# Attention and expert routing on one core: batch 1's q and k projected in three periods, the last x pass two periods later, q's weights applied after the turn, and a ten-round threshold search

## The reference

```python
xn = _layernorm(x, axis=-1)                       # x: 16 x 512 x 256
x = x + attention(xn) + ffn(xn)

# attention: 16 heads of 16, q and k with an RMS norm and a learned weight
q = rms_norm(proj(Wq), qn_w); k = rms_norm(proj(Wk), kn_w); v = proj(Wv)
attn = softmax(einsum('bhnd,bhmd->bhnm', q, k) * scale)
out = einsum('bhnm,bhmd->bhnd', attn, v) @ Wo.T

# ffn: 8 experts; each takes the C = T // 8 best of the tokens that are left
norm = layer_norm(feat, ln_g, ln_b); scores = norm @ centroids.T
for e in range(E):
    s = where(taken, -inf, scores[:, e]); _, idx = top_k(s, C); taken[idx] = True
routed = feat[concatenated idx]; h = layer_norm(routed, ln_g, ln_b)
h = gelu(h @ w1[e] + b1[e]) @ w2[e] + b2[e]       # 256 -> 1024 -> 256
out = routed + h, put back at each token's place
```

## Time and profile before

| | |
|---|---|
| three runs | 1201.72, 1202.34, 1205.91 us; median 1202.34 |
| the profiled execution | 1197.54 us, its span 1195.8 us |
| PE | 1063.0 us busy (89%) |
| DVE, ACT, POOL | 801.6 us (67%), 747.8 us (63%), 737.7 us (62%) |
| first block | to about 765 us |

### The profile page before, as it was taken

The page is one execution under the profiler, slowest core; times in us unless marked ns, Lnnn a source line. Parts: engine busy times, 40 slices in busy tenths (PEclk is TensorE's granted clock), DMA queues, the critical chain, the costliest instruction groups (busy, mean ns, idle before and its releaser), DMA issues. The chain is left out here.

```text
span 1195.8 us, 20979 instructions
## 1 busy us (share of the span) xinstructions
PE 1063.0 (89%) x7286; PEld 693.9 (58%) x7286; DVE 801.6 (67%) x1836; ACT 747.8 (63%) x966; POOL 737.7 (62%) x798
## 2 busy tenths in 40 slices
PE   4394999889999999999999999379999999999997
PEld 3251545445444444544454435268888888888887
DVE  6263687647787878687868778166676767667573
ACT  1173778678888878887888777154454444555442
POOL 5756679837667766776677631326665666655662
PEclk9697999989999999999999999679999999999999
DMA  3736687567686767667857680322424424243232
GB/s 113 165 66 150 113 201 159 127 127 141 138 155 154 125 139 163 147 130 148 159 153 127 147 166 19 128 76 46 123 49 111 110 41 124 45 119 83 64 45 27
DMA packets 84042, 138.17 MB, mean 116 GB/s; under 512 B 12496, under 2 KB 38352, under 8 KB 81872
## 3 DMA queue, kind: packets, MB, share of 16 engines
q1 hardware_dynamic: 56064, 104.63, 39.6%
q0 software_dynamic: 12288, 16.79, 8.6%
q10 hardware_dynamic: 15568, 15.21, 4.9%
HBM read 86.25 MB, written 50.33 MB: 114 GB/s over the span
## 5 line engine op out<-in xcount | busy, mean ns | idle before, releaser
L551 ACT ACTIVATE prob<-S 128x1024 f32<-128x1024 f32 x512 | 498.5, 1022 | 147.2 <-PE S L392 146.3
L392 PE MATMUL S<-stq,stk 64*128 64x512 f32 x1024 | 200.0, 458 | 55.8 <-DMA stk<-parts 40.4
L407 PE MATMUL pv<-prob,v 128*17 128x512 f32 x2048 | 247.3, 600 | 1.3 <-DVE oT L666 1.2
L1166 PE MATMUL dn<-w,hid 128*128 128x256 f32 x1536 | 194.1, 285 | 7.4 <-DVE hid L1332 7.2
L1166 PEld LDWEIGHTS dn<-w,hid 128*128 128x128 f32 x1536 | 188.1, 192 | 11.7 <-DVE hid L1332 10.0
L1154 PE MATMUL up<-nT,w 128*128 128x512 f32 x768 | 180.9, 395 | 12.8 <-DVE w L1268 10.5
L392 PEld LDWEIGHTS S<-stq,stk 64*128 64x128 f32 x1024 | 83.8, 186 | 180.3 <-ACT prob L551 111.2
L1154 PEld LDWEIGHTS up<-nT,w 128*128 128x128 f32 x768 | 145.2, 191 | 44.6 <-DVE w L1268 11.9
L1232 ACT ACTIVATE act<-up,b 128x512 f32<-128x512 f32 x128 | 87.9, 687 | 125.2 <-PE up L1154 124.1
L1393 POOL DMA_INDIRECT out<-y,order_rows x64 | 108.0, 1687 | 47.1 <-DVE y L1340 33.7
L951 POOL TENSOR_TENSOR sq<-raw 128x512 f32<-128x512 f32 x64 | 66.6, 1042 | 100.0 <-DVE raw L637 65.2
(11 more groups left out here) (167 smaller groups left out, 1819.0 us busy)
## 6 DMA issues: line engine op xcount, KB each, us to landing
stq<-parts SPq DMA_DIRECT2D x192, 128.0 KB, 5.2
stk<-parts SPq DMA_DIRECT2D x192, 128.0 KB, 6.2
parts<-hi SPq DMA_DIRECT2D x64, 256.0 KB, 2.3
parts<-lo SPq DMA_DIRECT2D x64, 256.0 KB, 2.4
out<-ao ACTq DMA_DIRECT2D x32, 256.0 KB, 5.0
w1raw<-in_w SPq DMA_DIRECT2D x8, 1024.0 KB, 7.0
w2raw<-in_w SPq DMA_DIRECT2D x8, 1024.0 KB, 4.8
xb<-in_x ACTq DMA_DIRECT2D x13, 512.0 KB, 4.3
```

The source lines that it names most:

```text
L392: ins = e.matmul(S[n % 2][:, h, :], stack["k"][u][64 * h:64 * h + 64, p, c * P:(c + 1) * P], stack["q"][u][64 * h:64 * h + 64, p, :], star ...
L407: ins = e.matmul(pv[32 * j:32 * j + VW, :], v[b % 2][:, c, 8 * u + 4 * g + j, :], prob[(2 * t + j // 2) % RING][:, j % 2, :], start=(c == ...
L551: e.activation(prob[n % RING][:, :, :], S[n % 2][:, :, :], ACT.Exp).then_inc(s_exp, 1)
L1166: ins = e.matmul(down[c % 2][:, 0:D], hid[ph][:, fc, c * P:(c + 1) * P], w2[pw][:, fc, :], start=(fc == 0 and i == 0), stop=(fc == NFC - 1 ...
```

## The change

Four edits to the first block:

1. Batch 1's q and k projections stand in periods 0, 0, 1, 2 in place of 0, 1, 2, 3, its v projections in 3 and 4 in place of 4 and 5; the sum of squares of its first half moves from period 3 to 1, and with it scale, turn and split of that half by two periods. At the start POOL splits x of batch 1 ahead of scaling batch 0's second half.
2. The x pass of batch 15 stands in periods 28 to 31 in place of 26 to 29.
3. q's weights are no longer multiplied in on POOL ahead of the turn (L960, 512 elements against a row), but behind it, as one number per partition (a TENSOR_SCALAR on half of `full`, in `split_qk`). A ninth constant is loaded at the start, and DVE computes one more small column.
4. The search has ten rounds: two of 4 bits (15 candidates, so `ge` is 960 wide) and eight of 3 bits. An expert takes 11 periods in place of 12, so the last period of search is 108, `rest` stands in 109, and the order work in periods 111 to 118, with `keep_order` in 119. Its one-hot tiles lie in `xT` and `xb`.

```diff
-BITS = 3
-CAND = 2 ** BITS - 1
...
+ROUND_BITS = (4, 4, 3, 3, 3, 3, 3, 3, 3, 3)
+HIGH_STEPS = 5
+STEPS = len(ROUND_BITS)
...
+ORDER = ROUTE + (E - 1) * ROUNDS + 2
...
 def scored(at):
-    m = SCORE_FROM + at // 2
-    return m if at >= 0 and at % 2 == 0 and m < B else None
+    if at == 2 * (B - SCORE_FROM):
+        return B - 1
+    return SCORE_FROM + at // 2 if at in range(0, 2 * (B - 1 - SCORE_FROM), 2) else None
...
     if nb == 1:
-        return i
+        return (0, 0, 1, 2)[i]
...
-    return 4 + i if nb == 1 else PERIODS * (nb - 1) + 2 + i
+    return 3 + i if nb == 1 else PERIODS * (nb - 1) + 2 + i
...
-    return qk_at(nb, 1) + 2 if u == 0 else PERIODS * (nb - 1) + 5
+    return PERIODS * (nb - 1) + (1, 5)[u]
...
-                    if nb == B:
-                        order_tensor(e, kk)
+                    if 0 <= at - ORDER < PERIODS:
+                        order_tensor(e, at - ORDER)
...
-            e.scalar_tensor_tensor(ge[:, :, :], key.unsqueeze(1).broadcast_to([P, CAND, NT]), best[:, 0:1],
...
+            e.scalar_tensor_tensor(ge[:, 0:CAND[i], :], key.unsqueeze(1).broadcast_to([P, CAND[i], NT]), best[:, 0:1],
...
-                    if nb == B:
-                        order_columns(e, kk)
+                    if 0 <= at - ORDER < PERIODS:
+                        order_columns(e, at - ORDER)
+                    if at - ORDER == PERIODS:
+                        keep_order(e)
...
-            e.wait_ge(s_rk, 2 * n + 1)
-            e.tensor_tensor(q, q, wq_row[:, :].unsqueeze(1).broadcast_to([P, 32, DH]), ALU.mult).then_inc(s_rq, 1)
...
+            e.tensor_scalar(full[:, 0, :], full[:, 0, :], wq_col[:, 0:1], None, ALU.mult).then_inc(s_wq, 1)
+            e.wait_ge(s_wq, n + 1)
             e.tensor_copy(hi[:, :, :], full[:, :, :]).then_inc(s_hi, 1)
```

More of the change, by code:

```diff
@@ L29 @@
 SAFE_BOUND = 60.0
-BITS = 3
-CAND = 2 ** BITS - 1
-LOW_BITS = 14
-HIGH_STEPS = (32 - LOW_BITS) // BITS
-LOW_STEPS = -(-LOW_BITS // BITS)
-STEPS = HIGH_STEPS + LOW_STEPS
+ROUND_BITS = (4, 4, 3, 3, 3, 3, 3, 3, 3, 3)
+HIGH_STEPS = 5
+STEPS = len(ROUND_BITS)
+LOW_BITS = sum(ROUND_BITS[HIGH_STEPS:])
+CAND = [2 ** b - 1 for b in ROUND_BITS]
+MOST = max(CAND)
 UNIT = 2.0 ** (LOW_BITS + 1)
@@ L38 @@
 TAKEN = -2.0 ** 21 * UNIT
-STEP = [UNIT * 2.0 ** (BITS * i) for i in reversed(range(HIGH_STEPS))] + [2.0 ** (BITS * i) for i in reversed(range(LOW_STEPS))]
+STEP = [(UNIT if i < HIGH_STEPS else 1.0) * 2.0 ** sum(ROUND_BITS[i + 1:HIGH_STEPS if i < HIGH_STEPS else STEPS])
+        for i in range(STEPS)]
 PRODUCTS = ((0, 0), (0, 1), (1, 0))
@@ L164, in attention_and_routing @@
         below = sb("below", [P, P], BF16)
-        cand = sb("cand", [P, STEPS, CAND])
+        cand = sb("cand", [P, STEPS, MOST])
         best = sb("best", [P, 1])
         digit = sb("digit", [P, 1])
-        ge = sb("ge", [P, CAND, NT], BF16)
-        part_cnt = sb("part_cnt", [P, CAND], BF16)
-        gem = sb("gem", [P, CAND])
+        ge = sb("ge", [P, MOST, NT], BF16)
+        part_cnt = sb("part_cnt", [P, MOST], BF16)
+        gem = sb("gem", [P, MOST])
         gt = sb("gt", [P, NT], BF16)
@@ L202, in attention_and_routing @@
             sem(f"s_{n}") for n in ("bn", "mv", "ln", "xn", "turn", "xT", "sc", "sT", "sm", "score", "xh", "xl"))
-        s_proj, s_raw, s_sq, s_ssq, s_lg, s_rs, s_rk, s_rq, s_full, s_hi, s_lo, s_hi_out, s_lo_out = (
-            sem(f"s_{n}") for n in ("proj", "raw", "sq", "ssq", "lg", "rs", "rk", "rq", "full", "hi", "lo", "hi_out", "lo_out"))
+        s_proj, s_raw, s_sq, s_ssq, s_lg, s_rs, s_rk, s_wq, s_full, s_hi, s_lo, s_hi_out, s_lo_out = (
+            sem(f"s_{n}") for n in ("proj", "raw", "sq", "ssq", "lg", "rs", "rk", "wq", "full", "hi", "lo", "hi_out", "lo_out"))
         s_stack = [sem(f"s_stack{u}") for u in range(2)]
@@ L219, in attention_and_routing @@
         offb = sq[:, 0, 0:KD * P].rearrange("p (d f) -> p d f", d=KD)
-        hot_p = [raw[i][:, :, :].rearrange("p n t -> p (n t)").rearrange("p (t q) -> p t q", t=COLS) for i in range(2)]
-        hot_t = [sq[:, i, :].rearrange("p (t q) -> p t q", t=COLS) for i in range(2)]
+        hot_p = [xT[8 + i][:, :, :].rearrange("p d t -> p (d t)").rearrange("p (t q) -> p t q", t=COLS) for i in range(2)]
+        hot_t = [xb[i][:, 0:2, :].rearrange("p c d -> p (c d)").rearrange("p (t q) -> p t q", t=COLS) for i in range(2)]
         word = xb[0][:, 0:2, :].rearrange("p c d -> p (c d)").bitcast(I32)
@@ L437, in route_tensor @@
                 e.wait_ge(r_pc, STEPS * ex + i + 1)
-                e.matmul(R[:, 0:CAND], ones_h[:, :], part_cnt[:, :], start=True, stop=True).then_inc(r_cnt, 1)
+                e.matmul(R[:, 0:CAND[i]], ones_h[:, :], part_cnt[:, 0:CAND[i]], start=True, stop=True).then_inc(r_cnt, 1)
             else:
@@ L733, in answer @@
             e.wait_ge(r_cnt, n + 1)
-            e.tensor_scalar(gem[:, :], R[:, 0:CAND], float(C), None, ALU.is_ge, ALU.add, accum_out=digit[:, :]).then_inc(r_dg, 1)
+            e.tensor_scalar(gem[:, 0:CAND[i]], R[:, 0:CAND[i]], float(C), None, ALU.is_ge, ALU.add, accum_out=digit[:, :]).then_inc(r_dg, 1)
             e.wait_ge(r_dg, n + 1)
@@ L801, in order_columns @@
                 e.wait_ge(r_last, 9)
+                e.wait_ge(s_xl, 20)
+                e.wait_ge(s_turn, 2 * B)
             if i >= 2:
@@ L1449 @@
     i = {n: np.asarray(v) for n, v in inputs.items()}
-    cand = np.array([[(c + 1) * s for c in range(CAND)] for s in STEP], np.float32)
+    cand = np.array([[(c + 1) * s for c in range(MOST)] for s in STEP], np.float32)
     arrays = {
@@ L1456 @@
         "wo": on_partitions(i["L0_attn_Wo"].T.reshape(KD, 2, 4, DH, D).transpose(0, 2, 1, 3, 4).reshape(D, D)),
-        "qk_row": np.broadcast_to(np.stack([i["L0_attn_qn_w"], i["L0_attn_kn_w"]])[None], (P, 2, DH)),
+        "qk_row": np.stack([i["L0_attn_qn_w"], i["L0_attn_kn_w"]])[None],
+        "qk_col": np.tile(np.stack([i["L0_attn_qn_w"], i["L0_attn_kn_w"]], 1), (P // DH, 1)),
         "centroids": on_partitions(i["L0_ffn_centroids"].T),
```

27 lines of the change are left out of this document (15 added, 12 removed).

## The result

The changed kernel takes 1229.12 us (median of four runs, 1227.04 to 1233.71), against 1202.03 for the kernel before: a ratio of 1.023, 95% interval 1.020 to 1.026. The forecast was 1207.2, in a range up to 1217. The profiled execution has a span 29.5 us longer than before's. A trace is one execution: before's took 1197.54 us, 4.5 under its median, and the changed kernel's 1227.04, 2.1 under. So a place that is a few us off between two traces need not come from an edit.

The account below looks back on a forecast made before the run. PE was taken to bound the first block, except at two large stalls. Terms -14.3 - 7.9 + 2.9 + 12.3 + 0.6 + 16.5 - 5.2 = +4.9 us on the median 1202.34 gave 1207.2, range 1195 to 1217.

Parts of the forecast that it names:

- q's weights: New POOL operation behind the turn, on the chain to the read-back, taken at 0.6 us: +0.6 us (0 to +1.5).
- Period 8: PE's 16.9 us stall for `stk` falls to 3 us and the clock stays up: -14.3 us (-17 to -11).
- the forecast of the tiles: Score tiles of period 8 start at 103.1 in place of 116.2, after the split ends at 89.3.
- Period 28: ACT's 10.0 us wait for a ring tile goes, 3.5 us remain at period 30: -7.9 us (-11.4 to -6).
- The 3.5 us wait at period 30: ACT still waits about 3.5 us there, on POOL's x split.
- Period 32: DVE's six passes start 1.9 us later and the wide question adds 1.05: +2.9 us (+1 to +4).
- The wide questions: 1.05 us more per question, two per expert; 2.05 reach PE for experts 1 to 6: +12.3 us (6.3 to 18).
- The order work: Added to full PE in periods 111 to 118, with DVE as long as PE: +16.5 us (+14 to +24).
- The last batch: Periods 118 to 127 shorten without order work, less two or three clock dips: -5.2 us (-10 to -1).
- a sign of its being wrong: Periods 120 to 127 at full clock throughout would show the prediction wrong.
- The rival of DVE as the bound: DVE bounds periods 111 to 118 as POOL's work meets its columns: 23.6 in place of 16.5 us, 1214; chance 0.27.

Follow-up runs that it names:

- one more line: Edits 1 and 2 alone, with POOL's x split of batch 5 moved from period 29 to 27: 1180.98 us, 0.983 of the kernel before.

## Why the prediction was wrong

**The step that failed is "q's weights": +0.6 us (0 to +1.5).** Measured alone, it is +22 us. It failed twice, in the price of the operation and in the count of the places where it is paid. The price: an operation that the trace did not hold was put at 0.6 us, near a cast, between bounds of 610 and 1287 ns; it takes 1571, above the upper one. The Trainium skill (GPSIMD Engine Reference, "Engine selection") calls one-input elementwise work on GpSimd roughly line-rate; the trace disagrees for this form, in which a two-input TENSOR_TENSOR over the same elements is the faster one. The count: I looked at POOL's load, found it no bound, and charged the chain once, at batch 2. But turn, scaling by the weights, `hi`, `lo`, write and read-back end ahead of the next half's tiles with little to spare in many places: before's trace already waits for the stack at periods 16, 24, 64, 88 and 112. In edit 3 alone the first four waits grow by 8.6 us together, 7 of the next 18 halves wait in place of 2, and the clock is at half in two more stretches and for longer at period 8. What was taken off ahead of the turn saved nothing against it. The forecast of the whole put 0.6 where 22 were measured; the other terms' misses are smaller, and in part cancel.

**Period 8 (-14.3)** was right but for that: -15.6 with edits 1 and 2 alone, tiles 1 us ahead of the forecast. In the changed kernel PE is 3.2 us behind at period 7 already (3.5 more than in that run), the split ends 3.5 us later, and the read-back takes 16.2 us, where the forecast had 12.9 and that run 14.1; the half clock costs the rest. In part the forecast of the tiles was luck: with edits 1 and 2 alone the split ended 2.2 us ahead of it (0.6 of that for the operation that is not there), and the read-back was 1.2 longer.

**Period 28 (-7.9).** The 3.5 us wait at period 30 was right, 3.46 without edit 3. What I left out is that behind the wait PE runs at half clock (period 30 took 11.1 us there and 12.8 in the changed kernel, 5.1 before), so 4.7 us were got, and 6.4 without edits 3 and 4.

**Period 32 (+2.9)** came out at +6.9, and at +5.1 without edits 3 and 4. It adds up so: the first pass starts 5.7 us into period 31, before 1.9, a slip of 3.8 where I had 1.9; passes and question take 8.9 us, before 7.2, of which the wide question has 1.1, and four passes of 1.06 to 1.51 us (before, three of 1.4) the rest; and period 33, partly at half clock behind PE's wait of 3.81 us, is 1.7 longer. That is 7.2, less 0.3 us that lay between DVE's end and PE's count before. The term was undersized.

**The wide questions (+12.3).** Alone, with the order work last, the search costs 15 us by its ratio, so the size was in the range, but by the traces the mechanism that I priced is the smaller part: 4 to 5 of 17.5 us in periods 37 to 109. The near hit of the sum is luck. I never asked what eleven periods an expert do to the place at which one ends: with twelve, starting at 32, the ties fall only on periods 0 and 4 of a batch; with eleven on 3, 6, 1, 4, 7 and 2. Rows 7 have only the good places.

**The order work (+16.5, 14 to 24)** was +20.2, in its range; the excess of 3.7 is about what the two stretches at half clock cost (3.4 us long, so 1.7 lost in each). **The last batch (-5.2)** was -9.9: no dips of the clock, which the prediction had named as a sign of its being wrong. The sum of the two, +11.3, was nearly right (9 and 11 measured) because the two misses cancel. The rival of DVE as the bound had this cause right, and it is a small part of the miss. The Trainium skill (TensorE: Matmul & The Clock Gate, "Why this matters for your kernels") asks that long idle gaps be kept out, and by that leaves the last batch at full clock, and the trace agrees: 4.8 us a period at 1.00.

The parts do not add up: -13 (edits 1, 2), +22, +15 and +11 make 35, and the whole is 27. That a stall absorbs lateness ahead of it would explain some of this, and each number carries 3 to 5 us; which edits overlap where was not shown. What stays open is what decides whether the clock falls: in the changed kernel it fell behind a wait of 1.91 us (period 112) and not behind one of 1.86 us (period 48, where the score tiles behind take the usual 0.73) or even of 3.29 us (period 24), and no run was made to separate them.

## What to carry to other kernels

An edit that is "off the bound engine" is priced by every chain it stands in: count how often the chain runs and how much it has to spare where it ends, ask whether time saved at another point of the chain can reach its end, and take an operation that the trace doesn't hold at its upper bound or above. A loop whose length is changed moves its expensive end through another loop's phases; write down where each end falls. Edits that come together should be costed, and tried, apart: two of these are worth 13 us, with one more line 20.
